# Wide attention: slots two by two, and the maximum over partitions on GpSimd

## The reference, cut to what matters

```python
q = _split_heads(jnp.einsum('bnd,df->bnf', x, Wq))
kv = jnp.einsum('bmc,cf->bmf', context, Wkv)
k, v = jnp.split(kv, 2, axis=-1)
...
k = jnp.concatenate((nk, k), axis=-2)
v = jnp.concatenate((nv, v), axis=-2)
q = q * scale
sim = jnp.einsum('bhid,bhjd->bhij', q, k)
attn = jax.nn.softmax(sim, axis=-1)
out = jnp.einsum('bhij,bhjd->bhid', attn, v)
out = out.transpose(0, 2, 1, 3).reshape(b, -1, INNER)
out = jnp.einsum('bnf,fd->bnd', out, Wout)
```

## Time and profile before

| | us |
|---|---|
| median of 3 runs | 5164.85 (5157.47 to 5165.71) |
| profiled execution | 5157.35 |
| its span, first to last instruction | 5155.5 |
| PE busy | 4166.4 (81%) |
| DVE busy | 3516.8 (68%) |
| ACT busy | 2516.7 (49%) |
| POOL busy | 1357.4 (26%) |
| POOL additions at L2988, 768 of them | 1111.2 |

### The profile page before, as it was taken

One profiled execution on the slowest core, in us unless ns is written; L12 is line 12 of the kernel. 1 busy time (PEld: TensorE's weight loads), 2 busy tenths in 40 slices (PEclk: granted clock), 3 DMA queues, 4 the chain that ended last, 5 costly groups with the idle time before them and its releaser, 6 DMA issues. The chain is left out here.

```text
span 5155.5 us, 77653 instructions
## 1 busy us (share of the span) xinstructions
PE 4166.4 (81%) x29315; PEld 2196.3 (43%) x29315; DVE 3516.8 (68%) x5424; ACT 2516.7 (49%) x3542; POOL 1357.4 (26%) x1033
## 2 busy tenths in 40 slices
PE   5740596999999999999995995876996768888872
PEld 3530234656666666665652332432443332222221
DVE  5379444777777777777785444766773548888867
ACT  2120242666666666666662222543664345766762
POOL 0000300566565656566664502000000100000000
PEclk5565797999999999999996997987997688999986
DMA  0010001000000000000002206305650333323200
GB/s 18 1 59 0 0 0 50 1 14 1 14 1 14 14 1 14 1 14 1 1 1 96 89 0 147 52 15 99 82 78 4 89 61 67 53 43 51 47 2 8
DMA packets 135603, 167.70 MB, mean 33 GB/s; under 512 B 19498, under 2 KB 108092, under 8 KB 134676
## 3 DMA queue, kind: packets, MB, share of 16 engines
q1 hardware_dynamic: 127540, 146.39, 14.0%
q0 software_dynamic: 6528, 16.42, 1.3%
q10 hardware_dynamic: 1184, 0.12, 0.0%
HBM read 125.31 MB, written 34.55 MB: 31 GB/s over the span
## 5 line engine op out<-in xcount | busy, mean ns | idle before, releaser
L2988 POOL TENSOR_TENSOR arena<-arena 128x512 f32<-128x512 f32 (+1 forms) x768 | 1111.2, 1447 | 756.0 <-ACT arena L2944 716.5
L2443 ACT ACTIVATE arena<-ps 128x1024 f32<-128x1024 f32 (+1 forms) x688 | 703.2, 1023 | 329.7 <-PE ps L2368 319.1
L3035 DVE TENSOR_TENSOR arena<-arena 128x1024 f32<-128x1024 f32 (+1 forms) x448 | 707.5, 1580 | 24.2 <-ACT arena L2971 24.2
L2461 DVE TENSOR_REDUCE arena<-ps 128x2 f32<-128x826 f32 (+1 forms) x576 | 564.5, 980 | 185.4 <-PE ps L2314 176.9
L2937 ACT ACTIVATE arena<-ps 128x1024 f32<-128x1024 f32 (+1 forms) x448 | 431.1, 962 | 327.0 <-PE ps L2862 326.9
L3011 DVE TENSOR_TENSOR arena<-ps,arena 128x512 f32<-128x512 f32 (+1 forms) x768 | 527.9, 687 | 86.5 <-ACT arena L2937 68.2
L2314 PE MATMUL ps<-arena 48*128 48x413 bf16 (+3 forms) x1920 | 433.7, 332 | 132.2 <-DVE arena L2461 64.4
L2862 PE MATMUL ps<-arena 64*128 64x256 f32 (+1 forms) x3328 | 477.3, 402 | 0.7 <-ACT arena L2960 0.7
L2876 PE MATMUL ps<-arena 128*64 128x256 f32 (+1 forms) x3328 | 459.3, 394 | 7.3 <-ACT arena L2944 7.2
L2846 PE MATMUL ps<-arena 128*128 128x256 f32 (+1 forms) x1664 | 462.6, 399 | 0.0
L2944 ACT ACTIVATE arena<-arena 128x1024 f32<-128x1024 f32 (+1 forms) x448 | 441.4, 985 | 19.4 <-DVE arena L3035 16.4
(11 more groups left out here) (645 smaller groups left out, 5949.3 us busy)
## 6 DMA issues: line engine op xcount, KB each, us to landing
arena<-ctx_parts SPq DMA_DIRECT2D x96, 200.1 KB
arena<-ctx_parts SPq DMA_DIRECT2D x192, 100.1 KB
arena<-in_ctx_feat SPq DMA_DIRECT2D x8, 1601.0 KB, 6.4
arena<-in_ctx SPq DMA_DIRECT2D x16, 768.0 KB
arena<-diff_att_stack SPq DMA_DIRECT2D x60, 192.0 KB
ctx_parts<-arena SPq DMA_DIRECT2D x24, 400.2 KB, 3.6
arena<-in_w SPq DMA_DIRECT2D x1, 6416.0 KB, 18.5
arena<-in_ctx_feat SPq DMA_DIRECT2D x8, 800.5 KB
```

The source lines that it names most:

```text
L2443: act.activation(self.prob[0:rows, u % 3, :], self.ps[0:rows, 2 * (u % 2):2 * (u % 2) + 2, :].rearrange("p n c -> p (n c)"), ACT.Exp).then ...
L2461: ins = dve.tensor_reduce(dst[:, :, j // 2], self.ps[:, 4:6, 0:hi - lo], AX.X, ALU.max)
L2988: pool.tensor_tensor(acc[0:rows, u % 2, :], before, sc[0:rows, u % 2, t, :], ALU.add).then_inc(added, 1)
L3035: dve.tensor_tensor(x, x, mb[0:rows, u % 2, None, :].to_broadcast([rows, n, 2 * S]), ALU.subtract).then_inc(sub_done, 1)
```

## The change

Three things are done together.

1. All loops of the stage take two slots at a time: scores of both, then values of both, then the ring's keys of both. DVE subtracts for two slots, then takes the maxima of the two slots of the same pass (it ran one slot behind before). ACT copies two, then takes two exponentials, which it now does with the subtraction's own lag (`LAG` - 2, before one slot more). The sums and the normalization of a unit come in the same pass, with `LAG` + 2.
2. "turn" and "bcast", with `mx`, the reduction at L3022 and the copy at L2971, are gone.
3. In their place POOL issues, once per unit, `partition_all_reduce` with the maximum, from `top` straight to `mb`, 512 columns. For unit 0 it stands ahead of all additions, for unit u + 1 behind the additions of slot k = 3 of unit u. DVE waits for it (`max_all`) before the first subtraction of the unit, and before it overwrites `top`.

```diff
-        self.first, self.end = -self.STEPS, self.SLOTS + self.LAG + 4
+        self.first, self.end = -self.STEPS - 1, self.SLOTS + self.LAG + 8
...
-            for s in range(plan.first, plan.end):
-                if plan.unit(s):
-                    scores(s, *plan.unit(s))
-                if plan.unit(s, plan.LAG):
-                    values(s - plan.LAG, *plan.unit(s, plan.LAG))
+            for s in range(plan.first, plan.end, 2):
+                for slot in plan.pair(s):
+                    scores(*slot)
+                for slot in plan.pair(s, plan.LAG):
+                    values(*slot)
...
-                    elif key[0] == "turn":
-                        pe.wait_ge(max_done, len(tiles) * (key[1] + 1))
-                        bank = ring_bank(key)
-                        for j in range(4):
-                            ins = pe.transpose(ps[:, bank, j * P:(j + 1) * P], top[:, key[1] % 2, j * P:(j + 1) * P],
-                                               ident[:, :])
-                        ins.then_inc(ring_ready, 1)
-                    elif key[0] == "bcast":
-                        wait_copied(pe, ("turn", key[1]))
-                        bank = ring_bank(key)
-                        for j in range(4):
-                            ins = pe.matmul(ps[:, bank, j * P:(j + 1) * P], mx[:, j:j + 1].to_broadcast([P, P]),
-                                            ident[:, :], start=True, stop=True)
-                        ins.then_inc(ring_ready, 1)
...
-                done = plan.unit(s, plan.LAG + 1)
-                if done and done[1] == plan.STEPS - 1:
-                    u = done[0]
+                for u in plan.ended(s, plan.LAG + 2):
...
-                if plan.unit(s, plan.LAG - 1):
-                    u, k = plan.unit(s, plan.LAG - 1)
+                for x, u, k in plan.pair(s, plan.LAG - 2):
                     n = len(plan.tiles_of(k))
                     rows = tiles[2 * k][1]
-                    act.wait_ge(sub_done, s - plan.LAG + 2)
-                    x = sc[0:rows, u % 2, 2 * k:2 * k + n, :]
-                    act.activation(x, x, ACT.Exp).then_inc(exp_done, 1)
+                    act.wait_ge(sub_done, x + 1)
+                    e = sc[0:rows, u % 2, 2 * k:2 * k + n, :]
+                    act.activation(e, e, ACT.Exp).then_inc(exp_done, 1)
...
-                    else:
-                        u = key[1]
-                        if u >= 2:
-                            act.wait_ge(sub_done, plan.STEPS * (u - 1))
-                        act.activation(mb[:, u % 2, :], ps[:, bank, :], ACT.Copy).then_inc(ring_act, 1)
...
+            def spread(u):
+                pool.wait_ge(max_done, len(tiles) * (u + 1))
+                if u >= 2:
+                    pool.wait_ge(sub_done, plan.STEPS * (u - 1))
+                pool.partition_all_reduce(mb[:, u % 2, :], top[:, u % 2, :], P, bass.bass_isa.ReduceOp.max
+                                          ).then_inc(max_all, 1)
+            spread(0)
             for s in range(plan.SLOTS):
...
+                if k == 3 and u + 1 < plan.UNITS:
+                    spread(u + 1)
...
+                for x, u, k in plan.pair(s, plan.LAG - 2):
+                    n = len(plan.tiles_of(k))
+                    rows = tiles[2 * k][1]
+                    if k == 0:
+                        dve.wait_ge(max_all, u + 1)
+                    e = sc[0:rows, u % 2, 2 * k:2 * k + n, :]
+                    dve.tensor_tensor(e, e, mb[0:rows, u % 2, None, :].to_broadcast([rows, n, 2 * S]), ALU.subtract
+                                      ).then_inc(sub_done, 1)
+                for x, u, k in plan.pair(s):
+                    dve.wait_ge(s_copied, x + 1)
```

More of the change, by code:

```diff
@@ L2723, in __init__ @@
         self.chunks = list(zip(cut[:-1], cut[1:]))
-        self.first, self.end = -self.STEPS, self.SLOTS + self.LAG + 4
+        self.first, self.end = -self.STEPS - 1, self.SLOTS + self.LAG + 8
         self.index, self.act_count, self.dve_count = {}, {}, {}
         n = a = d = 0
-        for s in range(self.first, self.end):
+        for s in range(self.first, self.end, 2):
             for key in self.ring_of(s):
@@ L2730, in __init__ @@
                 n += 1
-                if key[0] in ("q", "k", "v", "bcast"):
+                if key[0] in ("q", "k", "v"):
                     a += 1
@@ L2746, in ring_of, with pair, ended @@
     def ring_of(self, s):
[L2748 to L2763, removed]
+        keys, late = [], []
+        for x in (s, s + 1):
+            u, k = divmod(x, self.STEPS)
+            if u + 1 < self.UNITS and k == 0:
+                keys.append(("q", u + 1))
+            if 0 <= x < self.SLOTS and x % 14 < len(self.tiles):
+                keys.append(("v", x // 14, x % 14))
+            if u + 1 < self.UNITS and k in self.CHUNK_AT:
+                keys.append(("k", u + 1, self.CHUNK_AT[k]))
+            last = x - self.LAG - 5 - 6
+            if last >= 0 and last % (self.STEPS * HP) == self.STEPS * (HP - 1):
+                late.append(("out", last // (self.STEPS * HP)))
+        return keys + late
+    def pair(self, s, lag=0):
+        return [(x - lag, *self.unit(x, lag)) for x in (s, s + 1) if self.unit(x, lag)]
+    def ended(self, s, lag):
+        return [u for _, u, k in self.pair(s, lag) if k == self.STEPS - 1]
 def stage4(env):
@@ L2780, in stage4 @@
         top = st.sb("top", [P, 2, 2 * S])
-        mx = st.sb("mx", [P, 4])
         mb = st.sb("mb", [P, 2, 2 * S])
@@ L2790, in stage4 @@
         st_ready, s_copied, max_done = st.sem("st_ready"), st.sem("s_copied"), st.sem("max_done")
+        max_all = st.sem("max_all")
         sub_done, exp_done, added = st.sem("sub_done"), st.sem("exp_done"), st.sem("added")
@@ L2925, in _ @@
             act.wait_ge(null_moved, 32)
-            for s in range(plan.first, plan.end):
-                if plan.unit(s):
-                    u, k = plan.unit(s)
+            for s in range(plan.first, plan.end, 2):
+                for x, u, k in plan.pair(s):
                     n = len(plan.tiles_of(k))
                     rows = tiles[2 * k][1]
-                    act.wait_ge(st_ready, s + 1)
+                    act.wait_ge(st_ready, x + 1)
                     if u >= 2:
-                        act.wait_ge(pv_done, s - 2 * plan.STEPS + 1)
+                        act.wait_ge(pv_done, x - 2 * plan.STEPS + 1)
                         act.wait_ge(added, last_tile * (u - 2) + plan.tiles_of(k)[-1])
-                    src = ps[0:rows, 2 + 2 * (s % 2):4 + 2 * (s % 2), 0:n * S].rearrange("p e (j q) -> p e j q", j=n)
+                    src = ps[0:rows, 2 + 2 * (x % 2):4 + 2 * (x % 2), 0:n * S].rearrange("p e (j q) -> p e j q", j=n)
                     dst = sc[0:rows, u % 2, 2 * k:2 * k + n, :].rearrange("p j (e q) -> p e j q", e=2)
                     act.activation(dst, src, ACT.Copy).then_inc(s_copied, 1)
-                if plan.unit(s, plan.LAG - 1):
-                    u, k = plan.unit(s, plan.LAG - 1)
+                for x, u, k in plan.pair(s, plan.LAG - 2):
                     n = len(plan.tiles_of(k))
                     rows = tiles[2 * k][1]
-                    act.wait_ge(sub_done, s - plan.LAG + 2)
-                    x = sc[0:rows, u % 2, 2 * k:2 * k + n, :]
-                    act.activation(x, x, ACT.Exp).then_inc(exp_done, 1)
+                    act.wait_ge(sub_done, x + 1)
+                    e = sc[0:rows, u % 2, 2 * k:2 * k + n, :]
+                    act.activation(e, e, ACT.Exp).then_inc(exp_done, 1)
                 for key in plan.ring_of(s):
@@ L2996, in _ @@
             ins.then_inc(null_k_ready, 1)
[L2997 to L3000, removed]
+            for s in range(plan.first, plan.end, 2):
+                for x, u, k in plan.pair(s, plan.LAG - 2):
[6 more added lines that the diff above has]
+                                      ).then_inc(sub_done, 1)
+                for x, u, k in plan.pair(s):
+                    dve.wait_ge(s_copied, x + 1)
                     for t in plan.tiles_of(k):
                         rows = tiles[t][1]
-                        got = ps[0:rows, 2 + 2 * ((s - 1) % 2):4 + 2 * ((s - 1) % 2), t % 2 * S:(t % 2 + 1) * S]
+                        got = ps[0:rows, 2 + 2 * (x % 2):4 + 2 * (x % 2), t % 2 * S:(t % 2 + 1) * S]
                         most = top[0:rows, u % 2, :].rearrange("p (e q) -> p e q", e=2)
@@ L3006, in _ @@
                             if u >= 2:
-                                dve.wait_ge(ring_ready, plan.index["turn", u - 2] + 1)
+                                dve.wait_ge(max_all, u - 1)
                             ins = dve.tensor_copy(most, got)
@@ L3013, in _ @@
                 for key in plan.ring_of(s):
[L3014 to L3024, removed]
-                        b = key[1]
[L3026 to L3039, removed]
+                    if key[0] == "out":
+                        b = key[1]
+                        dve.wait_ge(ring_ready, plan.index[key] + 1)
```

(3 more changed lines are left out.)

## The result

| | before | changed |
|---|---|---|
| median of 4 runs | 5161.57 us (5157.47 to 5165.71) | 5506.43 us (5503.12 to 5521.05) |
| profiled execution, its span | 5157.35, 5155.5 us | 5503.12, 5501.2 us |

The change makes the kernel slower: the ratio is 1.068, with a 95% interval of 1.065 to 1.071 (the plain quotient of the medians is 1.067); the medians lie 345 us apart, the two profiled executions 346. The forecast was slower too, with POOL as the bound through its loads, but by 734 us, more than double. The time lies in the stated range, at its lower side.

What follows compares the result with a forecast made beforehand. PE bounds the kernel before, POOL the changed one: additions 17.8, loads 13.2, maximum 9 make 40.0 us a unit; 63 periods x 11.6 = 731, with head and tail +734 on 5157.4, forecast 5890 us, range 5300 to 7200.

Steps and rivals of the forecast that it cites:

- That POOL becomes the bound through loads: Wide attention: POOL needs 40.0 us a unit against PE's 25.95, with two code loads in it; forecast mechanism's chance 0.78.
- the load term: POOL's two code loads per unit, into the maximum and back into additions: 6.6 us each, 13.2 together; bounds 0 to 13.4.
- The maximum's own time: POOL's all-partition maximum on 512 columns: 9 us per unit, geometric middle of bounds 0.6 and 128 us.
- head: Stage's start, from unit 0's last maximum to its first subtraction: 7.9 us before, about 9 + 1 after, so +2.
- tail: Stage's end on POOL: one load and 17 additions after the last maximum, 36 us against some 35, so +1.
- Saturated "within a us or two": POOL's queue around each maximum: load and five old-unit additions cover the wait for new exponentials, within a us or two.
- Parts 1 and 2: PE per unit: removed transposes and broadcast save 1.32 us, slots in pairs 1.16; period 28.43 falls to 25.95 us.
- reordering: Slots in pairs: new order costed at nothing, covered by DVE's 5 us idle a unit, or up to 1 us.
- Rival A: POOL's maximum: columns hardly overlap, nearly 0.25 us each, about 13,500 us in all; chance 0.16 for above 30 us.
- Rival B: POOL's maximum is nearly free, 0.6 to 3 us, only loads count: 5357 to 5510 us; chance 0.20, inside the forecast.
- Rival C: POOL's loads are not paid again, so PE's 25.95 us a unit sets the time: 4999 us, faster; chance 0.04.
- Rival D: PE is throttled or pair order stalls: adds at most 190 us, held in the range; no chance of its own.

Runs made afterwards that it cites:

- e4: Kernel before plus one unread one-column all-partition maximum on GpSimd per unit, behind the additions of k = 3; transposes and broadcast stay; 5453.08 us, ratio 1.057.
- e1: Changed kernel with a plain GpSimd copy of 512 columns from top to mb in place of the all-partition maximum; 5033.15 us, ratio 0.977.
- e6: Changed kernel with the all-partition maximum one slot earlier in POOL's queue, behind the additions of k = 2 instead of k = 3; 5546.65 us, ratio 1.078.
- e2: Changed kernel's slots in pairs, but the maximum over partitions by TensorE's transposes and broadcast as before, none on POOL; 5096.12 us, ratio 0.988.
- e5: Changed kernel with the all-partition maximum issued twice in a row, the second from mb to mb; 5622.47 us, ratio 1.093.

## Why the prediction was right or wrong

**That POOL becomes the bound through loads: right.** e4 adds the loads and a maximum of 0.38 us to the kernel before and pays 295 us; e1 has everything else without the loads and the maximum and gains 125. The bound below of the load term, "a second load is free", is excluded: both were paid in every unit (the first one under the wait at the stage's start), 5.9 us into the maximum and 7.2 into the additions, 13.1 in place of 13.2. They were paid at each change and not once in the program: in e4 the shortest of the 64 gaps was 5.7 us before the maximum and 6.6 before the additions.

**The maximum's own time: the step that failed.** The prediction took 9 us, the geometric middle of 0.6 and 128; it is 1.80 us. One column takes 0.35 and 512 take 1.80, so a further column adds 1.45 / 511 = 2.8 ns, near the 2.5 ns of an addition (1.27 us for 512). The upper bound had taken 0.25 us of the instruction on one column as a price per column, where these two durations show it to be nearly all a price of the instruction, paid once; and the middle between a fixed price and a price per column has no meaning of its own. 7.2 us too much, 64 times, is 461 us. The nearest row in kind was the GpSimd pass over as many columns, not the same instruction on one. Put in place of the 9, the prediction's own sum gives 17.8 + 13.2 + 1.8 = 32.8 us, 63 x 4.37 = 275, a head shorter by 5 and 1 at the tail: 5428 us. That is 75 us short of the profiled 5503, the other way.

**Saturated "within a us or two": right, but counted at nothing.** POOL waits 1.1 us a unit for exponentials, additions with their hand-overs are 0.3 us over their term (18.1 against 17.8), and the loads 0.1 under theirs: 34.13 against 32.8 is 1.3 us, 84 us in 63 periods. That closes the gap of 75 us but for the head and the 7 us of the stages behind. What makes the wait stays open. ScalarE's copies of scores wait for POOL's additions of two units before, which free `sc`, exponentials stand behind these copies in its queue, and POOL waits for them:

```profile
L2925 ACT ACTIVATE arena<-ps 128x1024 f32<-128x1024 f32 (+1 forms) x448 | 417.1, 961 | 573.8 <-POOL arena L2978 374.1
```

That these 374 us lead to POOL's 1.1 us a unit is argued; e6, which was to show it, showed only that the place of the maximum behind k = 3 isn't the cause.

**Parts 1 and 2, work off PE: right in size.** 2.48 us a unit were worked out from distances of starts; e1's PE does 25.98 us a unit in place of 28.43. e2 shows the half for the pairs: 27.62 x 0.987 = 27.3 us of PE's work, 1.2 less than before, where 1.16 was forecast; of this the period kept 0.8, as reordering, which was counted at nothing, brought 0.4 us of waits. In the changed kernel this gain exists and is worth nothing as such, since PE waits.

**Rival A: it did not come.** A further column costs 2.8 ns and not 0.25 us. **Rival B** (0.6 to 3 us, 5357 to 5510) was the case that came, with a fifth of the chance, where it should have been the likeliest. **Rival C** did not come, as the loads were paid again, but its price was near: with neither loads nor maximum the changed order is at 5033 us, where 4999 was said.

**Rival D, the clock.** The granted clock fell from 1.00 to 0.91 in the window above and 0.90 in others, and PE now stands still up to 8 us at a time. The level shows in its timeline: the same four instructions take double the time behind a wait.

```profile
1605.49 3.03 PE L2843 MATMUL ps<-arena 128*128 128x400 f32 x4 [6.36 <-ACT arena L2953]
...
1612.92 1.50 PE L2843 MATMUL ps<-arena 128*128 128x400 f32 x4
```

The granted clock was 0.50 from 1605.4 to 1608.6 us, around the four that took 3.03 us, and 1.00 from 1612.9 to 1614.5, where they took 1.50. POOL's period is the sum above, and in it the clock shows directly only in the 1.1 us of waiting, at most 69 us in 63 periods, where the prediction allowed 190; no run separates its part.

## What to carry to other kernels

Before an operation is moved to GpSimd, look in the trace for the configuration instruction that stands ahead of it and of its neighbours: where two kinds of code alternate, each change cost 5.9 or 7.2 us here, of an engine that the busy share shows as idle, and no less for a short operation: e4 paid 5.9 and 7.0 us around one of 0.38. Price an operation on many columns by rows of passes over as many columns and not by its time on one column, and where two bounds lie far apart, forecast for the mechanism of each end and not for their middle. And when a change has two parts, time them apart: the pairs alone gave 1.2%, which the change as a whole hid behind a loss of 7%. An addition on GpSimd was not of one length either, 1.27 us in the mean beside no subtraction of VectorE and 1.78 beside one in the changed kernel: see in the trace which instructions of VectorE it ran beside before its duration is put into a sum.

## What the runs showed of the hardware

- The all-partition maximum takes 0.35 us for one column of 128 partitions (before, L4296) and 1.80 us for 512 (changed).
- A change of GpSimd between additions and the all-partition maximum costs 5.7 to 6.3 us into the maximum and 6.6 to 7.7 us into additions (shortest and longest of e4). It does so although, in the changed kernel's timeline, GpSimd's last addition had ended only 7.6 us before the load that brings additions back, and its last maximum 27.4 us before the next load. A copy between additions (0.61 us, 1.6 beside a subtraction) costs no load (e1).
- A GpSimd addition of 512 columns takes 1.25 to 1.29 us beside no subtraction of VectorE (all eight traces), and 1.51 to 1.85 us in the mean beside one, by run (1.78 in the changed kernel). The all-partition maximum goes from 1.80 up to 2.8 us (e6).
- DVE's first subtraction, in the timeline of the changed kernel below, starts 0.03 us after the end of the maximum that began at 1623.52, and e5's two maxima start 1.90 us apart, so the profiled span of this instruction, 1.80 us, is near its real one.

```profile
1625.35 1.22 DVE L2996 TENSOR_TENSOR arena<-arena 128x1024 f32<-128x1024 f32 x1 [1.98 <-POOL arena L2963]
```
